# Last batch of attention spread over rows by TensorE, and five groups of the last norm on ScalarE

## The reference

```python
x = _layernorm(x + _L0_attn_ref(x, Wq, Wk, Wv, Wu, Wo))               # linear attention, 16 heads
x = _layernorm(x + _L0_xattn_ref(x, ctx, mask, mask, Wq, bq, ...))    # softmax attention over ctx
x = _layernorm(x + _L0_ffn_ref(x, router, gate_up, down, ...))        # top 4 of 16 experts
```

```python
dot = jnp.einsum('bhdt,bhds->bhts', q, k) / math.sqrt(HEAD_DIM)
mask = target_mask[:, :, :, None] * source_mask[:, :, None, :]
dot = mask * dot - (1.0 - mask) * NEG
amap = jax.nn.softmax(dot, axis=-1) * mask
out = jnp.einsum('bhts,bhds->bhdt', amap, v)
```

## Time and profile before

| | |
|---|---|
| median of 3 runs | 1651.98 us (1651.69 to 1657.13) |
| the profiled execution | 1652.93 us, its span 1650.7 us |
| mean granted TensorE clock | 0.951 of full |
| block `attention` ends, `route` starts | about 816.3 and 816.8 us |
| block `last_norm` | 1622.5 us to the end |

### The profile page before, as it was taken

One profiled execution on the slowest core, in us unless ns is written; L12 is line 12 of the kernel. 1 busy time (PEld: TensorE's weight loads), 2 busy tenths in 40 slices (PEclk: granted clock), 3 DMA queues, 4 the chain that ended last, 5 costly groups with the idle time before them and its releaser, 6 DMA issues. The chain is left out here.

```text
span 1650.7 us, 28337 instructions
## 1 busy us (share of the span) xinstructions
PE 1470.6 (89%) x7422; PEld 1027.6 (62%) x7423; DVE 950.9 (58%) x1379; ACT 710.3 (43%) x1328; POOL 806.6 (49%) x650
## 2 busy tenths in 40 slices
PE   6988989889999999998256999999999999999990
PEld 5767767634444444442145878778787878877770
DVE  2333242677787778784294555555555555555555
ACT  4212121157777777777123234434434434444220
POOL 4424242443456545644333466666666576486322
PEclk9999999989999999999577999999999999999995
DMA  6101003264665475541362455565556565373326
GB/s 214 49 26 47 13 13 56 47 102 67 108 118 106 80 130 103 86 83 40 101 249 71 103 149 143 154 152 143 155 141 159 133 177 152 98 192 79 58 57 211
DMA packets 93712, 180.13 MB, mean 109 GB/s; under 512 B 17576, under 2 KB 20392, under 8 KB 93000
## 3 DMA queue, kind: packets, MB, share of 16 engines
q1 hardware_dynamic: 73944, 133.88, 31.8%
q0 software_dynamic: 18544, 44.84, 13.6%
q10 hardware_dynamic: 1152, 0.52, 0.2%
HBM read 115.55 MB, written 33.49 MB: 90 GB/s over the span
## 5 line engine op out<-in xcount | busy, mean ns | idle before, releaser
L824 DVE TENSOR_REDUCE stage<-ps_a 128x2 f32<-128x1024 f32 x256 | 300.5, 1218 | 87.9 <-PE ps_a L1045 87.3
L1600 POOL TENSOR_TENSOR we_split<-we_raw,we_split 128x512 f32 (+1 forms) x192 | 250.5, 1543 | 98.7 <-ACT we_split L1591 97.0
L638 ACT ACTIVATE probs<-ps_b 128x512 f32<-128x512 f32 x512 | 277.9, 595 | 43.6 <-PE ps_b L1060 41.3
L1885 PE MATMUL ps_y<-we_split,hT 128*128 x912 | 234.2, 406 | 4.0 <-DVE hT L1816 3.3
L1885 PE MATMUL ps_g<-we_split,xT 128*128 x912 | 230.6, 402 | 5.1 <-issue 4.2
L1885 PE MATMUL ps_u<-we_split,xT 128*128 x912 | 231.9, 403 | 0.0
L1885 PEld LDWEIGHTS ps_g<-we_split,xT 128*128 128x128 f32 x912 | 171.8, 190 | 53.1 <-issue 13.0
L1885 PEld LDWEIGHTS ps_y<-we_split,hT 128*128 128x128 f32 x912 | 167.8, 190 | 41.7 <-issue 6.3
L1885 PEld LDWEIGHTS ps_u<-we_split,xT 128*128 128x128 f32 x912 | 166.7, 189 | 35.0
L1701 POOL DMA_INDIRECT scratch_acc<-x_keep,to_rows x76 | 121.2, 1594 | 110.6 <-issue 50.8
L1751 ACT ACTIVATE hT<-ps_h 128x512 fp32r<-128x512 f32 x76 | 45.3, 596 | 296.0 <-PE ps_h L1866 296.0
(11 more groups left out here) (214 smaller groups left out, 2114.6 us busy)
## 6 DMA issues: line engine op xcount, KB each, us to landing
we_raw<-in_w_expert SPq DMA_DIRECT2D x192, 256.0 KB, 3.0
stack<-xT_raw SPq DMA_DIRECT2D x192, 128.0 KB, 5.4
we_bias<-in_b_expert SPq DMA_DIRECT2D x16, 768.0 KB, 4.0
stage<-in_w SPq DMA_DIRECT2D x5, 1024.0 KB, 4.8
xT_raw<-in_xT SPq DMA_DIRECT2D x4, 1024.0 KB, 6.3
x_tok<-in_x POOLq DMA_DIRECT2D x16, 256.0 KB, 3.0
late<-o_pair SPq DMA_DIRECT2D x128, 32.0 KB
late<-scratch_inv SPq DMA_DIRECT2D x16, 256.0 KB
```

Of the source, the lines that this page charges most:

```text
L638: nc.scalar.activation(probs[:, n % 3, h], src[:], ACT.Exp, scale=DH ** -0.5).then_inc(b_kept, 1)
L824: nc.vector.tensor_reduce(out[:, :, i, k % NC], ps_a[i][:], AX.X, ALU.max, negate=True).then_inc(a_kept[i], 1)
L1600: nc.gpsimd.tensor_tensor(lo, W["raw"][:, k, c], hi, ALU.subtract).then_inc(W["lo"], 1)
L1885: mm = nc.tensor.matmul(out[:], left[:, a, c], w[:, bass.ds(par, 1), k, b, c].squeeze(1), start=(n == 0), stop=(n == len(passes) - 1))
```

## The change

In the last batch the numerators and denominators are no longer moved by DMA. VectorE builds a 0/1 matrix `head_rows` of two 128x64 halves from the identity (in the buffer of `kv_mask`, which is free by then). For each group of heads TensorE multiplies `o_all` by both halves in float32 (`spread_heads`), so that the 16 rows of numerators and the 16 equal rows of denominators of each head come out in 64 rows of `ps_a`; this stands at s = 8, 10, 14 and after the loop. VectorE inverts the denominators as 64x512, four times (`invert_spread`), and does for each half what GpSimd did (`add_spread`, `last_moments`, `last_norm`); GpSimd keeps only the power. VectorE also applies the norm of batch 6. Turns and logits move: turns of batch 5 from s = 8, 9 to s = 4, 5, its logits from behind the loop to s = 6, turns of batch 6 from behind the loop to s = 14, 15; the last logits are made half by half. The inverse of batch 6 moves from s = 7 to s = 4. Semaphores are renamed and merged accordingly (`heads_step` counts six steps a batch for what were three semaphores).

In `last_norm` groups 0 to 4 are normed by ScalarE in two passes (subtract the mean in place, then scale into `res`), for which VectorE makes the negated mean; groups 5 to 7 stay on VectorE.

```diff
+head_rows = kv_mask[:].rearrange("p (z m) -> p z m", z=2)
...
+    if b == B - 1:
+        return {4: [("turn", 2 * b - 4)], 5: [("turn", 2 * b - 3)], 6: [("logits", b - 2)],
+                14: [("turn", 2 * b - 2)], 15: [("turn", 2 * b - 1)]}.get(s, [])
...
-    order.append(("logits", B - 3))
-    for b in (B - 2, B - 1):
-        order += [("turn", 2 * b), ("turn", 2 * b + 1), ("logits", b)]
+    order += [("logits", B - 2), ("turn", NT - 2), ("turn", NT - 1), ("logits", B - 1)]
     return {use: i for i, use in enumerate(order)}, early
 USE, EARLY = uses_of_ring()
+LAST_STEPS = (7, 13)
...
-    for b in range(B):
+    for b in range(B - 1):
...
-    move_heads(NG * B - 1)
-    store_inv(B - 1)
-    load_inv(B - 1)
+    move_heads(NG * (B - 1) - 1)
+    store_inv(B - 2)
+    load_inv(B - 2)
+    store_x2(B - 3)
     store_x2(B - 2)
-    store_x2(B - 1)
-    sp.wait_ge(x2_stored, 16 * B)
+    for t in (NT - 2, NT - 1):
+        sp.wait_ge(last_step, LAST_STEPS[t - NT + 2])
+        sp.dma_start(S["x2"][t * P:t * P + P, :], x[:, t, :]).then_inc(x2_stored, 16)
+    sp.wait_ge(x2_stored, 16 * (B + 1))
...
-    normalize(B - 2)
-    finish_heads(B - 1)
-    normalize(B - 1)
+    pool.wait_ge(y2_moments, B - 1)
+    nc.gpsimd.tensor_tensor(rstd2[:], mean_var2[:, :, 1], minus_half2[:], ALU.pow).then_inc(y2_rstd, 1)
+    for o in range(2):
+        pool.wait_ge(y2_moments, B + o)
+        pool.wait_ge(x2_made, 2 * B - 2)
+        nc.gpsimd.tensor_tensor(rstd2[:, o:o + 1], mean_var2[:, o, 1:2], minus_half2[:, o:o + 1],
+                                ALU.pow).then_inc(y2_rstd, 1)
...
+        if G >= NG * B - 2:
+            act.wait_ge(heads_spread, 2 * (G % NG) - 2)
+        elif G >= 2:
             act.wait_ge(o_moved[G % 2], 80 * (G // 2))
         nc.scalar.activation(o_all[:, G % 2], ps_pv[:], ACT.Copy).then_inc(o_kept, 1)
...
-        if s in (8, 9) and b >= 2:
+        if s in (8, 9) and 2 <= b < B - 1:
             keep_turned(2 * (b - 2) + s - 8)
+        if s in (4, 5, 14, 15) and b == B - 1:
+            keep_turned(2 * b - 4 + (4, 5, 14, 15).index(s))
+        if s == 6 and b == B - 1:
+            keep_logits(b - 2)
         if s >= 12 and b + 2 < B:
             keep_qk(b + 2, (s - 12) // 2, s % 2)
     keep_o(NG * B - 1)
-    keep_logits(B - 3)
-    for b in (B - 2, B - 1):
-        keep_turned(2 * b)
-        keep_turned(2 * b + 1)
-        keep_logits(b)
+    keep_logits(B - 2)
+    keep_turned(NT - 2)
+    keep_turned(NT - 1)
+    keep_logits(B - 1)
...
+    def make_head_rows():
+        nc.vector.tensor_copy(head_rows.rearrange("p z (i d) -> p z i d", i=4),
+                              ident[:].rearrange("p (i z d) -> p z i d", i=4, z=2)).then_inc(last_step, 1)
+    def invert_spread(g):
+        rows = slice(64 * (g % 2), 64 * (g % 2) + 64)
+        dve.wait_ge(heads_spread, 2 * g + 1)
+        nc.vector.reciprocal(full[rows, g // 2], ps_a[g // 2][rows, 1]).then_inc(last_step, 1)
+    def add_spread(o):
+        b, at = B - 1, LAST_STEPS[o] - 5
+        inv_o, num_o = full[:, o], num_sb[:, b % 2, o]
+        dve.wait_ge(last_step, at + 1)
+        nc.vector.tensor_tensor(inv_o, inv_o, mask_in[b % 4], ALU.mult).then_inc(last_step, 1)
+        dve.wait_ge(last_step, at + 2)
+        dve.wait_ge(heads_spread, 4 * o + 4)
+        nc.vector.tensor_tensor(num_o, ps_a[o][:, 0], inv_o, ALU.mult).then_inc(last_step, 1)
+        dve.wait_ge(last_step, at + 3)
+        nc.vector.tensor_tensor(num_o, num_o, x[:, NT - 2 + o, :], ALU.add).then_inc(last_step, 1)
+    def last_moments(o):
+        b = B - 1
+        dve.wait_ge(last_step, LAST_STEPS[o] - 1)
+        nc.vector.bn_stats(stats2[:, o], num_sb[:, b % 2, o]).then_inc(y2_stats, 1)
+        dve.wait_ge(y2_stats, 4 * b + 2 * o + 1)
+        nc.vector.bn_aggr(mean_var2[:, o], stats2[:, o]).then_inc(y2_stats, 1)
+        dve.wait_ge(y2_stats, 4 * b + 2 * o + 2)
+        nc.vector.tensor_scalar(mean_var2[:, o, 1:2], mean_var2[:, o, 1:2], LN_EPS, None, ALU.add).then_inc(
+            y2_moments, 1)
+    def last_norm(b, o, made):
+        nc.vector.tensor_scalar(x[:, 2 * b + o, :], num_sb[:, b % 2, o], mean_var2[:, o, 0:1], rstd2[:, o:o + 1],
+                                ALU.subtract, ALU.mult).then_inc(made, 1)
...
-        if s == 7 and b >= 1:
+        if s == (4 if b == B - 1 else 7) and b >= 1:
             invert(b - 1)
+    make_head_rows()
+    invert_spread(0)
+    invert_spread(1)
     moments(B - 2)
-    invert(B - 1)
-    moments(B - 1)
+    dve.wait_ge(mask_loaded[(B - 1) % 4], 32)
+    dve.wait_ge(x2_made, 2 * B - 4)
+    add_spread(0)
+    dve.wait_ge(y2_rstd, B - 1)
+    for o in range(2):
+        last_norm(B - 2, o, x2_made)
+    dve.wait_ge(x2_made, 2 * B - 2)
+    last_moments(0)
+    dve.wait_ge(y2_rstd, B)
+    last_norm(B - 1, 0, last_step)
+    invert_spread(2)
+    invert_spread(3)
+    add_spread(1)
+    last_moments(1)
+    dve.wait_ge(y2_rstd, B + 1)
+    last_norm(B - 1, 1, last_step)
...
+    def spread_heads(G):
+        g = G % NG
+        rows = slice(64 * (g % 2), 64 * (g % 2) + 64)
+        pe.wait_ge(o_kept, G + 1)
+        if g == 0:
+            pe.wait_ge(last_step, 1)
+            for i in range(2):
+                pe.wait_ge(a_kept[i], N)
+        for z in (1, 0):
+            nc.tensor.matmul(ps_a[g // 2][rows, z], head_rows[:, z], o_all[:, G % 2], start=True,
+                             stop=True).then_inc(heads_spread, 1)
     def turn_x2(t):
-        pe.wait_ge(x2_made, t + 1)
+        if t >= NT - 2:
+            pe.wait_ge(last_step, LAST_STEPS[t - NT + 2])
+        else:
+            pe.wait_ge(x2_made, t + 1)
         out = bank("turn", t)
         for c in range(KC):
             mm = nc.tensor.transpose(out[:, c * P:(c + 1) * P], x[:, t, c * P:(c + 1) * P], ident[:])
         mm.then_inc(b_made, 1)
-    def logits(b):
+    def logits(b, tiles=(0, 1)):
         if b == 0:
             pe.wait_ge(R["loaded"], 80)
         out = bank("logits", b)
-        pe.wait_ge(b_kept, USE["turn", 2 * b + 1] + 1)
-        for i in range(2):
+        for i in tiles:
+            pe.wait_ge(b_kept, USE["turn", 2 * b + i] + 1)
             for c in range(KC):
                 mm = nc.tensor.matmul(out[:, i * E_:(i + 1) * E_], xT_r[:, i, c], R["w"][:, c, :],
                                       start=(c == 0), stop=(c == KC - 1))
-        mm.then_inc(b_made, 1)
+        if 1 in tiles:
+            mm.then_inc(b_made, 1)
...
-        if s in (8, 9) and b >= 2:
+        if s in (8, 9) and 2 <= b < B - 1:
             turn_x2(2 * (b - 2) + s - 8)
+        if s in (4, 5, 14, 15) and b == B - 1:
+            turn_x2(2 * b - 4 + (4, 5, 14, 15).index(s))
+        if s == 6 and b == B - 1:
+            logits(b - 2)
+        if s in (8, 10, 14) and b == B - 1:
+            spread_heads(NG * b + (8, 10, 14).index(s))
         if s >= 12 and b + 2 < B:
             project_qk(b + 2, (s - 12) // 2, s % 2)
     values(N - 2)
     values(N - 1)
-    logits(B - 3)
-    for b in (B - 2, B - 1):
-        turn_x2(2 * b)
-        turn_x2(2 * b + 1)
-        logits(b)
+    spread_heads(NG * B - 1)
+    logits(B - 2)
+    turn_x2(NT - 2)
+    logits(B - 1, (0,))
+    turn_x2(NT - 1)
+    logits(B - 1, (1,))
...
+ON_ACT = (0, 1, 2, 3, 4)
...
-        sp.wait_ge(normed, G4 * (g + 1))
+        sp.wait_ge(normed[g in ON_ACT], G4 * (g + 1 - (0 if g in ON_ACT else len(ON_ACT))))
...
+@block.scalar
+def _(act):
+    for g in ON_ACT:
+        act.wait_ge(less_mean, ON_ACT.index(g) + 1)
+        for t in range(G4 * g, G4 * g + G4):
+            nc.scalar.activation(acc[:, t], acc[:, t], ACT.Identity, bias=minus_mean[:, t:t + 1]).then_inc(
+                centred, 1)
+        act.wait_ge(rstd_made, g + 1)
+        act.wait_ge(centred, G4 * (ON_ACT.index(g) + 1))
+        for t in range(G4 * g, G4 * g + G4):
+            nc.scalar.activation(res[:, t], acc[:, t], ACT.Copy, scale=rstd[:, t:t + 1]).then_inc(normed[True], 1)
...
+        if g in ON_ACT:
+            nc.vector.tensor_scalar(minus_mean[:, ts], mean_var[:, ts, 0], -1.0, None, ALU.mult).then_inc(
+                less_mean, 1)
...
-        apply(g)
+        if g not in ON_ACT:
+            apply(g)
```

More of the change, by code:

```diff
@@ L215, in attention @@
         inv_made, inv_stored, inv_loaded = sem("inv_made"), sem("inv_stored"), sem("inv_loaded")
-        inv_masked, attn_scaled = sem("inv_masked"), sem("attn_scaled")
-        y2_added, y2_stats, y2_aggr, y2_moments, y2_rstd, x2_made, x2_stored = (
-            sem("y2_added"), sem("y2_stats"), sem("y2_aggr"), sem("y2_moments"), sem("y2_rstd"), sem("x2_made"),
+        heads_step, heads_spread, last_step = sem("heads_step"), sem("heads_spread"), sem("last_step")
+        y2_stats, y2_moments, y2_rstd, x2_made, x2_stored = (
+            sem("y2_stats"), sem("y2_moments"), sem("y2_rstd"), sem("x2_made"),
             sem("x2_stored"))
@@ L272, in load_mask @@
                 if b >= 4:
[L273 removed]
+                    sp.wait_ge(heads_step, 6 * (b - 4) + 2)
```

(35 more changed lines are left out.)

6 lines of the change are left out of this document (2 added, 4 removed).

## The result

The changed kernel takes 1638.2 us (median of 4 runs, 1637.33 to 1641.08) against 1652.89 (1651.69 to 1657.13, with one run more than before the prediction). The ratio is 0.991, 95% interval 0.9887 to 0.9932: 14.7 us, 0.9%, faster. The forecast was 1637.5. The profiled execution has a span of 1636.9 us, against 1650.7.

A forecast was written before the change was run, and what follows sets the result against it. TensorE was taken to bound nearly every slice, except attention's end and the last norm. Profiled 1652.93 minus 19.2 (chain) plus 8.6 (loop) minus 3.85 (last norm) gives 1638.5; median 0.95 lower, 1637.5 us; range 1631.5 to 1644.

The forecast's parts named there:

- The chain after the loop: From the last value product to VectorE's add ending the attention block: 14.4 us instead of 33.6, 19.2 less.
- The reciprocal: VectorE's inversion of 512 columns of denominators in the chain after the loop: 3.35 us, bounds 0.7 and 6.7.
- The loop: Last batch's attention steps: work added to TensorE ahead of the next scores makes them 8.6 us longer.
- logits at s = 6: Logits of batch 5 moved into the last batch's loop, with low-clock values after them: 2.9 us more.
- s = 8: wait and spread, against a plain step: Last batch's loop: spread costs 1.35 us, plus 0.65 waiting for VectorE's last maxima and head_rows.
- Turn at s = 14 not waiting for VectorE: Last batch's loop: VectorE norms batch 6 by 779.8, TensorE wants it at about 783; 3 us of cover.
- rival 2: Attention's end: reciprocal slower; at double price VectorE's chain passes its cover at s = 14, 1644.5 us; chance 0.07.
- The last norm: Kernel's end: ten instructions leave VectorE (4.5 us), five negated means come in (0.65); net 3.85 us less.
- the cover of ScalarE: Last norm: ScalarE, 2.4 us a group, ends five groups near 1640.5, 3 us of cover against VectorE.
- Rival 3: Last norm gains nothing, because stores and loads bound it or ScalarE's chain ends last: 1641.4 us; chance 0.10.
- Rival 1: Last batch's loop absorbs more: spreads cost 0.3 to 0.5 each, last turn and logits at 2.4 GHz: 1633; chance 0.20.
- Rival 4: Last batch's loop: clock stays at 1.2 GHz after the logits of s = 6, slower than before, 1660 us; chance 0.03.

The follow-up runs named there:

- changed_again: The changed kernel run once more with no edit, on the same chip as early_four; 1639.58 us, ratio 0.9927 to the kernel before.
- inverse_late: Changed kernel with the inverse of batch 6 back at s = 7 instead of s = 4; 1640.28 us, ratio 0.993 to the kernel before.
- rows_early: Changed kernel with make_head_rows at s = 4 of the last batch, ahead of VectorE's last maxima; 1632.97 us, ratio 0.9887 to the kernel before.
- attention_only: Changed kernel's attention with the last norm of the kernel before; 1638.39 us, ratio 0.9922 to the kernel before.
- norm_stores: Changed kernel with the last norm's store of group 5 issued ahead of that of group 4; 1637.68 us, ratio 0.9924 to the kernel before.
- turns_behind: rows_early with the logits of batch 5 and turns of batch 6 behind the loop again; 1636.35 us, one run.
- early_four: Changed kernel with make_head_rows at s = 4 and four last-norm groups on ScalarE instead of five; 1633.23 us, ratio 0.9884 to the kernel before.
- rows_early_2: Second run of rows_early, unchanged; 1635.25 us, ratio 0.989 to the kernel before.
- numerators_first: rows_early with the numerators' product ahead of the denominators' in each spread, the reciprocal waiting for the second; 1640.75 us, one run.

## Why the prediction was right, and where its terms were off

**The chain after the loop** was forecast at 14.4 us and took 14.35 in the changed kernel and in every variant that left it alone. The reciprocal was the term without a row: 6.1 ns a column from the earlier trace rows gave 3.35, and four of them took 3355 ns on average. That the source is PSUM and that there are 64 rows made no visible difference. The Trainium skill's repeat count of 8 ("VectorE: DVE Perf Modes", "Walkthrough: the 8-slice pipeline in each mode"), read as 8 cycles a column, would have made an estimated 4.4; the trace has 3.36, which at the same 0.96 GHz is near 6 cycles a column, so that reading was wrong. Two small terms were off against each other: moments to norm took 1.76 for 1.95, the spread 1.11 up to VectorE's start for 1.06. The last turn and logits did run at 1.2 GHz (1.11 and 1.86).

**The loop** was forecast to grow by 8.6 us and grew by 9.3, but by other terms than I had put (the last row also holds the shorter end of the loop):

| term | forecast | changed kernel |
|---|---|---|
| logits at s = 6 | 2.9 | 1.5 |
| s = 8: wait and spread, against a plain step | 2.0 | 4.9 |
| s = 10: spread | 1.35 | 1.0 |
| turns at s = 4, 5, 14, 15 less those of s = 8, 9, and the spread of s = 14 | 2.3 | 1.8 |

The sum came out because an over-estimate of 1.4 and some smaller ones met an under-estimate of 2.9; that is luck. The two products of a spread took 1.86, where I had put 2.12 by the products of 256 columns. In changed_again, where the step of s = 8 took 9.70, it grew by 11.7. The step that failed is the one on the wait at s = 8: "VectorE was through at 760.49, one small pass more makes 760.7". That row was from a kernel in which GpSimd was idle at that moment (from 749.59 to 768.39). The change itself moved the finish of batch 6 under it (I had worked out the new time of that finish, and had not asked who works beside it). inverse_late and rows_early show both halves of it: the small operations are slow by GpSimd's work, and the wait and the low clock go when `make_head_rows` is not behind them. The Trainium skill, "SBUF — State Buffer", "SBUF: two separate sides", has the rule: VectorE and GpSimd share a pair of ports, which one of them holds as an exclusive lock for a whole instruction. It binds a VectorE operation that uses both ports or has two inputs in SBUF, the latter only against a GpSimd operation that reads SBUF. The trace agrees: VectorE's two operations end at 762.39 and 763.62, and GpSimd's instructions of 1.27 us change at about 762.3 and 763.6. It spoke against this change, and I had left it out.

The other part of that step is the clock. A spread behind a wait of 2.4 to 3.9 us took 3.0 to 3.65 (s = 8 in changed, changed_again, attention_only and norm_stores; s = 14 in inverse_late, 3.45 behind 2.36), and at s = 8 after a wait of at most 1.04 it took 1.90 (the seven other traces). The one slow spread without such a wait is that of s = 14 in turns_behind, where the clock had fallen two steps before. I had priced a wait by its length alone.

The logits at s = 6 were followed by low-clock values in four of the nine traces that have them there (norm_stores, early_four, rows_early_2, numerators_first), where the step of s = 7 took 3.87 for 2.70; then the term is 2.7, close to my 2.9. So 2.9 was the dear end of a range of 1.5 to 2.7. After s = 0 it had happened in the trace of before, and I took one case for the rule.

**The covers.** Turn at s = 14 not waiting for VectorE: right, with 2.7 us to spare (normed tiles at 781.33, turn at 783.99). inverse_late shows what lies beyond: there the wait was 2.36, plus the clock. This was the mechanism of rival 2, met by another cause.

**The last norm** was forecast to give 3.85 and gave 1.8. VectorE's part came out a little better than forecast, 4.2 less (a negated mean delays the next operation by 0.07 to 0.08, not 0.13). The step that failed is the cover of ScalarE, "3 us of cover": I compared its last pass with VectorE's end, when the stores go out in the order of the groups and that of group 5 was ready 2.2 us before that of group 4. ScalarE needed 2.65 a group (1625.59 to 1628.24, passes of 0.71 from SBUF to SBUF), not 2.4. With the gaps that this leaves, the stores' rate became the bound; norm_stores and early_four win 1.1 of it back. Rival 3 was thus half true.

**The rivals.** Rival 1 (the loop absorbs more) didn't come; spreads cost 1.0 in a plain step. Rival 4, slower by a lasting low clock, didn't come either, but in nine of the eleven traces steps at the low clock cost the loop between 1.3 and 4.2 us (estimated from the same steps at full clock), more often than I gave it credit for. That the whole was right to 0.7 us is largely luck. In the traces the parts that the change touches gave 11.8 us where 14.45 were forecast, and 2.0 us came from stretches without a change; in changed_again the touched parts gave 9.4. And the executions of one kernel that was timed more than once differ by 3.0 to 15.0 us.

## What to carry to other kernels

A DMA chain at the end of a stage, where nobody has other work, can be worth taking out even at the price of work on the busiest engine: here 19.3 us of chain were bought with 9.3 us of loop (11.7 in changed_again). When a step is moved earlier, look not only at who waits for it but at which instructions of the neighbouring engine run beside its new place, and put anything that TensorE waits for ahead of them. Where results of two engines leave by one queue in a fixed order, compare the readiness of each with its turn in the queue, not with the end of the stage.
